# Four graph layers on one core: a unit of the score pass with all four tiles in rounded products, and two high-part buffers for three

## The chip, the core and the metric

One Trainium2 chip, one of its cores. The metric is device time in microseconds (us) of one execution. The core has five engines with an instruction stream each: TensorE (PE, matmuls; its weight loads show as PEld), VectorE (DVE), ScalarE (ACT), GpSimd (POOL) and SyncE (SP, which here only issues DMA). An engine runs its stream in order, and the streams are tied together by semaphores that this kernel sets and waits for by hand.

## What is computed

`x` is 4096 nodes by 128 features, `adj` a 4096 x 4096 matrix. Four graph layers follow each other, each with a layer norm and relu ahead of it and a residual sum behind it. The change lies in the fourth. Its parts that matter:

```python
node_adj_norm = node_adj.at[idx, idx].add(-dn)            # adj without its diagonal
node_support = node_adj_norm @ h                          # 4096x4096 @ 4096x128, the node-feature product
edge_output = _gru_cell(node_support, h, edge_Wih, edge_Whh, edge_bih, edge_bhh)
# per attention head:
hp = (node_adj > 0) @ hW
hm = (node_adj < 0) @ hW
e_plus = leaky_relu(concat([hp, hm]) @ a); e_minus = leaky_relu(concat([hm, hp]) @ a)
...                                                       # softmax over columns, weighted sum, second gated cell
return de[:, None] * edge_output + dn[:, None] * node_output
```

## The kernel before

**Tiles.** The 4096 output columns are cut into C = 8 chunks of 512 (`c`), the 4096 rows summed over into G = 8 units (`g`) of four tiles of 128. A unit is one 1 MB block of `adj` (128 x 2048 float32: four tiles of 128 x 512), loaded by SP into one of the slots of `ring`. Unit number n = 8c + g. The passes over `adj` are: degrees, the first two layers (`agg0`, `agg1`), the third (`gat`), then for the fourth the **score pass** (`edge` in names), a normalising pass (`norm`) that reads stored masks, and the output pass (`out`). Only the score pass is touched.

**One unit of the score pass.** PE needs two products of the unit. The first, of the sign masks with a small table, is eight narrow matmuls (`L1693`). The second is the node-feature product: one tile of four (the first, `WHOLE = 1`) as a plain float32 matmul of `ring` with `reg1` (`L1700`, which the trace records as two instructions a tile), and three tiles as three rounded (fp32r) products each, high x high, low x high and high x low (`L1705`, `L1706`, `L1707`). The other engines make the operands:

- ACT `L694` (`sign_of`): the sign of 128 x 2048 elements, from which the masks are made, two units ahead.
- ACT `L709` (`high_parts`): a rounded copy of the tiles that are multiplied in rounded products, one unit ahead, into one of `HIGHS` buffers in `a_hi`.
- DVE `L1206` (`low_parts`): what the rounding left, unit minus high part, into `a_lo`, which lies over `ring`.
- DVE `L1191` and `L1194` (`masks`): plus and minus masks from the signs, two units ahead, into one of four buffers. SP stores them to HBM for the `norm` pass and loads the unit n + 6.

A high-part buffer comes free when PE has finished the unit that read it:

```python
if n >= HIGHS:
    act.wait_ge(s_mm["edge"], n - HIGHS + 1)      # L707, L708
act.activation(edge_hi(n), ring[...], ACT.Copy)   # L709
```

**Work beside the units.** For each finished chunk a chain of small steps is woven into the next chunk's units, at fixed places. ACT and DVE do in step n the high and low parts of unit n + 1 *first*, then the small steps, then signs and masks of unit n + 2:

- ACT at g = 1: `candidate` of chunk c - 1 (`L747`), then `keep_edge` of chunk c (`L729`, `L732`: sums out of the banks). At g = 7: two gate tanh (`L741`, `L742`).
- DVE at g = 0: `cell_in` (`L1231` to `L1233`); at g = 2: `edge_nodes` (`L1214` to `L1219`) and `cell_end` (`L1241` to `L1245`); at g = 4: `result` (`L1258`).
- PE behind unit g = 0: `turn_edge` (`L1716`), which waits for `L729`; behind g = 2: `turn_cells` (`L1503`), which waits for `L1245`; behind g = 4: `gates` (`L1731` to `L1734`), which waits for `L1258`.

`turn_edge` exists from chunk 1 on, the steps that work on the chunk before (`candidate`, `cell_in`, `cell_end`, `turn_cells`, `result`) from chunk 2 on. Chunk 0 has instead the rounding of `h` (`L705` on ACT, `L1202` on DVE), once per unit. On the diagonal unit (g = c) DVE also clears four 128 x 128 blocks (`L1169`). The order is written out by hand; no scheduler moves anything.

Of the kernel before, what the change touches and what calls it, by code (L numbers as in the profile page):

```python
# [34 lines left out]
VCOLS = 3 * HEADS * WINDOWS  # L35
ECOLS = 3 * 2 * HEADS + 1
EPAD = 32
WHOLE = 1
SCORES = 2 * HEADS
RING_EDGE = 6  # L40
RING_OUT = 4
MASKS = 4
MLOADS = 8
HIGHS = 3
TILES = 7
AHEAD = 2
EARLY = T - 2 * Q
# [51 lines left out]
def build(nc, x_d, rows_d, cols_d, diag_d, w_d, gru_d, col_d, row_d, masks_d, lines_d, xs_d, hs_d, out_d):  # L99
    with ExitStack() as ctx:  # L100
# [117 lines left out]
        signs = [b[:, 0:UNIT // 4] for b in (hT, outT)]  # L218
        SPLIT = (Q - WHOLE) * W

        def edge_hi(n):

            first = (MASKS - 1) * UNIT // 2 + (n % HIGHS) * SPLIT
            return a_hi[:, first:first + SPLIT]
# [147 lines left out]
        def ring_at(p, g, off=0, size=UNIT, c=0):  # L372
            slot = (c * G + g) % SLOTS[p]
            return slice(slot * UNIT + off, slot * UNIT + off + size)
# [159 lines left out]
        def _(act):  # L534
# [162 lines left out]
            def high_parts(n):  # L697
# [5 lines left out]
                if c == 0:  # L703
                    act.wait_ge(s_hkept, g + 1)
                    act.activation(h_hi[:, g * W:(g + 1) * W], reg1[:, g * W:(g + 1) * W],  # L705
                                   ACT.Copy).then_inc(s_hhi, 1)
                if n >= HIGHS:  # L707
                    act.wait_ge(s_mm["edge"], n - HIGHS + 1)  # L708
                act.activation(edge_hi(n), ring[:, ring_at("edge", g, WHOLE * W, SPLIT, c=c)],  # L709
                               ACT.Copy).then_inc(s_ehi, 1)  # L710
# [167 lines left out]
        def _(dve):  # L878
# [318 lines left out]
            def low_parts(n):  # L1197
# [6 lines left out]
                dve.wait_ge(s_ehi, n + 1)  # L1204
                rest = ring_at("edge", g, WHOLE * W, SPLIT, c=c)
                dve.tensor_tensor(a_lo[:, rest], ring[:, rest], edge_hi(n).bitcast(F32),  # L1206
# [292 lines left out]
        def _(pe):  # L1499
# [175 lines left out]
            def edge_unit(n):  # L1675
# [20 lines left out]
                for q in range(Q):  # L1696
                    t = g * Q + q
                    part, tile = ring_at("edge", g, q * W, W, c=c), slice(t * P, (t + 1) * P)
                    if q < WHOLE:
                        pe.matmul(nacc[:, :], reg1[:, tile], ring[:, part], start=t == 0, stop=False)  # L1700
                        continue
                    if q == WHOLE:
                        pe.wait_ge(s_elo, n + 1)
                    hi = edge_hi(n)[:, (q - WHOLE) * W:(q - WHOLE + 1) * W]
                    pe.matmul(nacc[:, :], h_hi[:, tile], hi, start=t == 0, stop=False)  # L1705
# [214 lines left out]
```

## Time and profile before

| | us |
|---|---|
| runs | 2068.22 (median of 3; 2066.27 to 2068.49) |
| the profiled execution | 2069.2 |
| its span, first to last instruction | 2067.4 |
| score pass within the span | from about 912 to 1205 |
| PE busy over the span | 1848.6 (89%) |
| DVE busy | 1662.5 (80%) |
| ACT busy | 1482.7 (72%) |

PE is the busiest engine, at a mean granted clock of 0.98. The stages have different limits, so the share over the span says little on a change to one stage; it is read from the score pass's own rows. In a row of the timeline the start and the duration of an instruction are given, and in brackets the idle time of its engine ahead of it with what ended it. Matmuls overlap: the pace of PE is the distance of two starts, not the duration of one.

### The profile page before, as it was taken

How to read it: one execution, taken by the hardware profiler on the slowest of the kernel's cores; microseconds unless marked ns; L12 is line 12 of the kernel's file. 1: busy time of each engine (PE TensorE's matmuls, PEld its weight loads, DVE VectorE, ACT ScalarE, POOL GpSimd, SP SyncE). 2: the span in 40 equal slices, each digit the busy share in tenths (PEclk: the TensorE clock that was granted, in tenths of full speed). 3: DMA queues.
4: the chain of work that ended last, by engine and by line, in shares of the span. 5: the costliest groups of instructions: out<-in, count | busy, mean ns of one | idle time of the engine just before them, and what ended most of it. 6: DMA issues, size and time to landing. Idle time of an engine off the chain costs nothing.

```text
span 2067.4 us, 22984 instructions
## 1 busy us (share of the span) xinstructions
PE 1848.6 (89%) x8237; PEld 1243.8 (60%) x8237; DVE 1662.5 (80%) x2326; ACT 1482.7 (72%) x1824; POOL 13.3 (1%) x15
## 2 busy tenths in 40 slices
PE   2335999789998999989999989989999999999998
PEld 1223888568887999975555546645555555554554
DVE  4658988698886888887887863399898898989987
ACT  3445666456667999988877730199898898988984
POOL 0000000000010000000000000000000000000000
PEclk9999999899998999989999999999999999999999
DMA  9999898578884776659998969723334333335230
GB/s 389 429 428 387 324 342 340 197 279 317 317 318 181 263 257 247 257 180 360 353 352 338 352 230 394 246 97 112 112 128 133 137 114 116 117 113 167 97 97 21
DMA packets 84161, 497.96 MB, mean 241 GB/s; under 512 B 8737, under 2 KB 12834, under 8 KB 38738
## 3 DMA queue, kind: packets, MB, share of 16 engines
q1 hardware_dynamic: 79730, 494.33, 63.8%
q10 hardware_dynamic: 4320, 2.20, 0.4%
q8 instruction: 64, 1.05, 0.2%
q14 instruction: 47, 0.39, 0.1%
HBM read 456.55 MB, written 39.94 MB: 240 GB/s over the span
## 4 chain that ended last, share of the span: by engine, by line
PE 60%; DVE 15%; ACT 11%; DMA 8%; issue 5%; SPq 0%; DVEq 0%; ACTq 0%
PE bank L1814 17%; DMA ring<-in_adj_rows 7%; PE bank L1626 5%; PE bank L1628 5%; PE bank L1627 5%; PE bank L1788 4%; ACT work L682 4%; ACT work L677 3%; PE bank L1700 2%; PE bank L1822 2%; PE bank L1821 2%; PE bank L1823 2%; DVE work L1468 2%; DMA ring<-masks 2%; DVE a_lo L1048 1%
## 5 line engine op out<-in xcount | busy, mean ns | idle before, releaser
L1814 PE MATMUL bank<-work,reg 128*128 128x512 f32 x760 | 362.0, 601 | 14.3 <-DVE ring L1419 7.9
L833 ACT ACTIVATE work<-x,e 128x512 f32<-128x512 f32 x552 | 355.1, 709 | 0.4 <-PE bank L1823 0.4
L1468 DVE TENSOR_TENSOR work<-work,ring 128x1536 f32<-128x1536 f32 x184 | 322.1, 1754 | 9.2 <-ACT work L833 9.0
L1048 DVE TENSOR_TENSOR a_lo<-ring,a_hi 128x2048 fp32r<-128x2048 f32 x128 | 292.5, 2302 | 30.9 <-ACT a_hi L626 30.1
L626 ACT ACTIVATE a_hi<-ring 128x2048 fp32r<-128x2048 f32 x128 | 244.3, 1913 | 77.1 <-PE bank L1628 77.1
L1660 PE MATMUL bank<-reg,ring 128*128 128x129 f32 x2048 | 244.4, 282 | 25.2 <-DVE ring L1162 24.8
L1660 PEld LDWEIGHTS bank<-reg,ring 128*128 128x128 f32 x2048 | 239.4, 197 | 29.5 <-DVE ring L1162 19.0
L1814 PEld LDWEIGHTS bank<-work,reg 128*128 128x128 f32 x760 | 143.6, 191 | 137.0 <-issue 112.8
L1626 PE MATMUL bank<-a_hi,s_hi 128*128 128x512 f32 x512 | 207.4, 405 | 20.5 <-DVE a_lo L1048 20.5
L1628 PE MATMUL bank<-a_hi,s_lo 128*128 128x512 f32 x512 | 202.1, 395 | 0.0
L1627 PE MATMUL bank<-a_lo,s_hi 128*128 128x512 f32 x512 | 200.8, 392 | 0.0
L1821 PE MATMUL bank<-s_lo,h_hi 128*128 128x512 f32 x240 | 189.1, 788 | 2.7 <-DVE a_lo L1447 2.4
L1162 DVE SCALAR_TENSOR_TENSOR ring<-ring,work 128x2048 f32<-128x2048 f32 x64 | 147.3, 2302 | 40.1 <-ACT work L682 40.0
L1447 DVE TENSOR_TENSOR a_hi<-work,s_lo 128x512 fp32r<-128x512 f32 x172 | 118.9, 691 | 42.0 <-ACT s_lo L843 41.8
L843 ACT ACTIVATE s_lo<-work 128x512 fp32r<-128x512 f32 x172 | 106.6, 620 | 55.9 <-PE bank L1823 39.0
L558 ACT ACTIVATE work<-ring 128x2048 f32<-128x2048 f32 x32 | 61.1, 1910 | 101.2 <-DMA ring<-in_adj_rows 101.2
L682 ACT ACTIVATE work<-work 128x2048 f32<-128x2048 f32 x64 | 122.4, 1912 | 14.1 <-DVE work L1131 8.4
L1206 DVE TENSOR_TENSOR a_lo<-ring,a_hi 128x1536 fp32r<-128x1536 f32 x64 | 112.4, 1756 | 21.4 <-ACT a_hi L709 19.1
L1626 PEld LDWEIGHTS bank<-a_hi,s_hi 128*128 128x128 f32 x512 | 97.4, 190 | 42.5 <-issue 24.2
L1788 PE MATMUL bank<-ring,work 128*126 128x512 fp8e4 x512 | 115.3, 383 | 5.7 <-issue 3.9
L709 ACT ACTIVATE a_hi<-ring 128x1536 fp32r<-128x1536 f32 x64 | 94.6, 1478 | 35.6 <-PE bank L1707 35.5
L1628 PEld LDWEIGHTS bank<-a_hi,s_lo 128*128 128x128 f32 x512 | 96.9, 189 | 22.8
(273 smaller groups left out, 3045.3 us busy)
## 6 DMA issues: line engine op xcount, KB each, us to landing
ring<-in_adj_units SPq DMA_DIRECT2D x320, 1024.0 KB, 4.9
ring<-in_adj_rows SPq DMA_DIRECT2D x32, 2048.0 KB, 17.0
ring<-masks SPq DMA_DIRECT2D x64, 512.0 KB, 5.1
masks<-work SPq DMA_DIRECT2D x48, 512.0 KB, 9.0
masks<-ring SPq DMA_DIRECT2D x16, 512.0 KB, 9.0
x<-lines SPq DMA_DIRECT2D x8, 768.0 KB, 9.8
ring<-lines SPq DMA_DIRECT2D x8, 768.0 KB, 8.0
h_kept<-reg SPq DMA_DIRECT2D x1, 2048.0 KB, 14.4
```

The costliest lines, as they stand in the source:

```text
L626: act.activation(a_hi[:, (g % 4) * UNIT:(g % 4 + 1) * UNIT], ring[:, ring_at(p, g)], ACT.Copy).then_inc(s_ahi[p], 1)
L682: act.activation(gunit(n), gunit(n), ACT.Exp).then_inc(s_gexp, 1)
L833: last = act.activation(tiles(n)[:, k * W:(k + 1) * W], guard(c, k), ACT.Sigmoid, bias=e6[:, t * SCORES + k:t * SCORES + k + 1], scale=-1.0)
L1048: dve.tensor_tensor(a_lo[:, ring_at(p, g)], ring[:, ring_at(p, g)], a_hi[:, (g % 4) * UNIT:(g % 4 + 1) * UNIT].bitcast(F32), ALU.subtract) ...
L1468: dve.tensor_tensor(tv, tv, spread(ring[:, ring_at("out", g, q * W, W)], HEADS, 1), ALU.mult).then_inc(s_y, 1)
L1626: pe.matmul(acc[:, :], sh, hi, start=begin, stop=False)
L1627: pe.matmul(acc[:, :], sh, lo, start=False, stop=False)
L1628: last = pe.matmul(acc[:, :], sl, hi, start=False, stop=end)
L1660: last = pe.matmul(gat_acc(c, i), y[:, q * W + i * P:q * W + (i + 1) * P], xw[:, m, :], start=m == 0 and i % 2 == 0, stop=m == T - 1 and i ...
L1788: last = pe.matmul(bank[c % 2][0:VCOLS, :], table[:, t * VCOLS:(t + 1) * VCOLS], mask[:, q * W:(q + 1) * W], start=t == 0 and table is vp, ...
L1814: return pe.matmul(bank[1 + k][:, :], reg1[:, t * P:(t + 1) * P], tiles(c * T + t)[:, k * W:(k + 1) * W], start=t == 0, stop=t == T - 1)
L1821: pe.matmul(acc, h_hi[:, h], high, start=t == 0, stop=False)
```

## The change

Two constants change:

```diff
-WHOLE = 1
+WHOLE = 0
...
-HIGHS = 3
+HIGHS = 2
```

`WHOLE = 0`: no tile goes through the plain float32 product any more; the high copy (`L709`) and the low part (`L1206`) cover 2048 columns in place of 1536, and PE makes 12 rounded products a unit in place of 9 and the plain one. The wait for the low part now stands ahead of the first tile (`if q == WHOLE: pe.wait_ge(s_elo, n + 1)`), and not behind the plain one. `HIGHS = 2`: two buffers of 2048 columns lie where three of 1536 lay (4096 columns in place of 4608), and the high copy of unit n waits until PE has finished unit n - 2, where it waited for unit n - 3.

On PE this is one unit of the score pass, before (-) and after (+); `a_hi` holds the high part of `adj`, `a_lo` its low part, `h_hi` and `h_lo` those of the features:

```order
 L1693 MATMUL bank<-work 32x512 x4
 L1693 MATMUL bank<-work,reg 32x512 x4
-L1700 MATMUL bank<-ring,reg 128x512
+L1705 MATMUL bank<-a_hi,h_hi 128x512
+L1706 MATMUL bank<-a_lo,h_hi 128x512
+L1707 MATMUL bank<-a_hi,h_lo 128x512
 L1705 MATMUL bank<-a_hi,h_hi 128x512
 L1706 MATMUL bank<-a_lo,h_hi 128x512
```

The plain product is gone from each of the 64 units, and three rounded ones stand in its place. All else on PE keeps its place.

On ACT these are the instructions around the head of a chunk (steps g = 0 and g = 1), first before:

```order
L709 ACTIVATE a_hi<-ring 128x1536 [waits edge_unit_multiplied]
L694 ACTIVATE hT<-ring 128x2048 [waits edge_masks_made,unit_loaded2]
L709 ACTIVATE a_hi<-ring 128x1536 [waits edge_unit_multiplied]
L747 ACTIVATE ring<-ring 128x512 [waits edge_gates_steps]
L729 ACTIVATE hn<-bank 128x512 [waits edge_sum_turned,edge_unit_multiplied]
L732 ACTIVATE ring<-bank 128x512 [waits edge_gates_multiplied]
```

and after:

```order
L709 ACTIVATE a_hi<-ring 128x2048 [waits edge_unit_multiplied]
L694 ACTIVATE hT<-ring 128x2048 [waits edge_masks_made,unit_loaded2]
L709 ACTIVATE a_hi<-ring 128x2048 [waits edge_unit_multiplied]
L747 ACTIVATE ring<-ring 128x512 [waits edge_gates_steps]
L729 ACTIVATE hn<-bank 128x512 [waits edge_sum_turned,edge_unit_multiplied]
L732 ACTIVATE ring<-bank 128x512 [waits edge_gates_multiplied]
```

Nothing moves on ACT (nor on DVE, where `L1206` alone grows to 2048 columns). What changes besides the width is a number that these rows don't show: the second `L709`, the copy for unit 8c + 2, waits for unit 8c in place of unit 8c - 1.

## Rows read from the trace of the kernel before

**Rows 1.** Stretch; busy us of PE, PEld, DVE, ACT, POOL; clock, DMA share, GB/s.
```profile
1016.00:1053.00 37.00, 36.64 (x186) 20.69 (x185) 28.67 (x43) 29.03 (x22) 0.00 (x0) 1.00 0.90 342
```

**Rows 2.** Groups by line, 905 to 1210: busy and mean ns, idle before, releaser.
```profile
L709 ACT ACTIVATE a_hi<-ring 128x1536 fp32r<-128x1536 f32 x64 | 94.6, 1478 | 35.6 <-PE bank L1707 35.5
```

**Rows 3.** Timeline of PE, one unit: start and duration in us.
```profile
1092.95 0.40 PE L1693 MATMUL bank<-ring,work 128*32 128x512 fp8e4 x4
1093.49 1.13 PE L1700 MATMUL bank<-ring,reg 128*128 128x512 f32 x2
...
1094.69 0.39 PE L1706 MATMUL bank<-a_lo,h_hi 128*128 128x512 f32 x1
...
1096.31 0.40 PE L1707 MATMUL bank<-a_hi,h_lo 128*128 128x512 f32 x1
1096.64 0.40 PE L1693 MATMUL bank<-work 128*32 128x512 fp8e4 x4
```

**Rows 4.** The page's costliest groups: the same operations at 2048 columns, in earlier passes.
```profile
L1048 DVE TENSOR_TENSOR a_lo<-ring,a_hi 128x2048 fp32r<-128x2048 f32 x128 | 292.5, 2302 | 30.9 <-ACT a_hi L626 30.1
L626 ACT ACTIVATE a_hi<-ring 128x2048 fp32r<-128x2048 f32 x128 | 244.3, 1913 | 77.1 <-PE bank L1628 77.1
```

**Rows 5.** Timeline of all engines at the head of chunk 5, then chunk 6.
```profile
1096.88 0.42 DVE L1231 TENSOR_SCALAR ring<-ring 128x512 f32<-128x512 f32 x1
1098.91 0.63 ACT L747 ACTIVATE ring<-ring 128x512 f32<-128x512 f32 x1 [0.56 <-DVE ring L1233]
1099.44 0.58 ACT L729 ACTIVATE hn<-bank 128x512 f32<-128x512 f32 x1
1100.24 0.96 PE L1716 MATMUL bank<-select,hn 128*128 128x19 f32 x8
...
1136.61 0.96 PE L1716 MATMUL bank<-select,hn 128*128 128x19 f32 x8
```

**Rows 6.** Timeline at units g = 2 and 3 of chunk 5.
```profile
1105.39 0.18 DVE L1214 COPY esum<-bank 128x24 f32<-128x24 f32 x1
1106.32 0.69 DVE L1241 TENSOR_TENSOR ring<-reg,ring 128x512 f32<-128x512 f32 x1
1108.38 0.42 DVE L1191 TENSOR_SCALAR work<-hT 128x512 int32<-128x512 int32 x1
1108.52 0.65 PE L1503 MATMUL bank<-ident,ring 128*128 128x128 f32 x4
```

**Rows 7.** Timeline at unit g = 4 of chunk 5 and the gates behind it.
```profile
1115.41 1.12 DVE L1258 SCALAR_TENSOR_TENSOR x<-bank,diag,x 128x128 f32<-128x128 f32 x4
1116.63 1.10 PE L1731 MATMUL bank<-ring,gru 128*128 128x512 f32 x2
1121.95 0.40 PE L1693 MATMUL bank<-work 128*32 128x512 fp8e4 x4
```

**Rows 8.** Timeline behind the gates of chunk 5: the high copy waits for PE.
```profile
1125.30 0.40 PE L1707 MATMUL bank<-a_hi,h_lo 128*128 128x512 f32 x1
1125.73 1.48 ACT L709 ACTIVATE a_hi<-ring 128x1536 fp32r<-128x1536 f32 x1 [3.88 <-PE bank L1707]
...
1128.26 1.91 ACT L694 ACTIVATE outT<-ring 128x2048 fp8e4<-128x2048 f32 x1
```

**Rows 9.** As rows 1: PE waits of 2.0 and 2.6 us, low stretches, full clock.
```profile
1367.65:1369.69 2.04, 0.00 (x1) 0.00 (x1) 2.04 (x3) 0.56 (x2) 0.00 (x0) 1.00 0.02 4
1370.96:1374.37 3.41, 3.41 (x7) 1.67 (x6) 3.41 (x5) 3.41 (x7) 0.00 (x0) 0.51 0.64 269
...
1343.06:1347.80 4.74, 0.00 (x0) 0.00 (x0) 1.75 (x1) 4.73 (x8) 0.00 (x0) 0.92 0.00 0
1348.90:1353.50 4.60, 4.60 (x8) 2.26 (x7) 4.00 (x5) 4.60 (x9) 0.00 (x0) 0.50 0.01 2
714.40:716.95 2.55, 0.00 (x0) 0.00 (x0) 2.52 (x5) 1.74 (x3) 0.00 (x0) 1.00 0.90 267
717.00:720.00 3.00, 3.00 (x27) 3.00 (x28) 3.00 (x4) 2.64 (x2) 0.00 (x0) 1.00 0.33 139
```

## Prediction, made before the changed kernel ran

> **What bounds the kernel now.** First the windows of the score pass, for the bound of this stage: in 37 us of it PE is busy 36.64, ACT 29.03 and DVE 28.67, at full clock and with the DMA engines at 0.90 [rows 1]. Then the groups by line, for the slack of the feeders: ACT's high copy stands idle 35.6 us over the stage, nearly all of it waiting for PE [rows 2]. So PE sets the pace and the feeders wait for it. Then the timeline of one unit on PE [rows 3]: from signs to signs 3.69 us; the plain tile and one rounded product take 1094.69 - 1093.49 = 1.20, and seven further products 1096.31 - 1094.69 = 1.62, so 0.231 each and 0.97 for the plain tile. Last the timeline at the three places where PE waits for a small step of another engine [rows 5 to 7], and behind the gates, where the copy waits for PE [rows 8]. A chunk lasts 1136.61 - 1100.24 = 36.4 us [rows 5].
>
> **What it removes.** 64 plain tiles of 0.97 become 64 times three products of 0.231: 0.27 saved a unit, 3.42 in place of 3.69. With PE alone that is 17.3 us.
>
> **What it adds on the feeders.** By the same operations at 2048 columns the copy takes 1.91 (1.48 now) and the low part 2.30 [rows 4], which at 1536 columns is about 1.76. ACT then has copy and signs, 3.6 us a unit (each next instruction starts 0.10 ahead of the end of the last one, as L729 behind L747 [rows 5]); DVE low part and masks, about 3.5. Both are now above PE's 3.42, but PE has 6.7 us of small steps a chunk besides (turn_edge, turn_cells, gates), so by sums alone the three are level near 34 us a chunk. Sums don't decide; the new wait does.
>
> **The new wait.** The copy of unit n + 2 may now start only when PE has finished unit n. From there to the products of n + 2: hand-over 0.03 (the end of L1707 to L709) [rows 8], copy 1.91, low part 2.30, hand-overs 0.1, so 4.3 us, and PE has unit n + 1 (3.42) and the signs of n + 2 (0.54) to do: it loses 0.4 where nothing lies between. That is the small part. The large part is queued behind the waiting copy. ACT and DVE run in order and do a unit's copy and low part ahead of the small steps, and these now start one unit later, while PE waits for them at the same place as before.
>
> I walked one chunk (c of 2 or more) with the durations above, t = 0 when ACT sees unit g = 4 of the chunk before as finished (0.43 behind the last product's start [rows 8]). In a steady state the gates start at 1.93 (third wait below) and last 5.3 [rows 7], so the signs of g = 5 start at 7.17, and this unit is finished at 10.69, g = 6 at 14.11.
>
> - g = 7 and g = 0. Copy of g = 7 at 10.69, low part done 14.94, products 0.45 late; finished 17.98. ACT is behind too: copy of g = 0 at 14.30, gates' tanh (2.53 from copy to signs less 1.38 [rows 8]), signs to 19.16. Low part of g = 0 done 18.55, products 0.19 late, finished 21.59.
> - **Turn_edge.** Copy of g = 1 at 19.06, its low part done 23.31, only then cell_in (23.23), and candidate 2.03 behind its start [rows 5], at 25.26. The copy of g = 2, which waited for the end of g = 0, stands ahead of it and is done at 24.59. Then L729, 25.79 to 26.37, and turn_edge at 26.41. PE could have started it at 21.39: 5.0 us idle. (Before, L1716 followed L729's end at 1100.02 by 0.2, with PE busy.) In chunk 1, without candidate, copy and L729 alone come to 2.6.
> - **Turn_cells.** Unit g = 1 is finished at 30.82; copy, low part to 35.07, edge_nodes 0.93 and cell_end 2.06 plus the tail of its last instruction [rows 6], PE at 38.12. PE was done with g = 2 at 34.14: 4.0 us idle.
> - **Gates.** g = 3 finished at 42.22; copy, low part to 46.47, result 1.12 [rows 7], gates at 47.57, where PE was free at 45.44: 2.1 us idle.
> - g = 4 is finished at 45.64. That is the new length of a chunk, 45.6 against 36.4.
>
> Clearing the diagonal falls where DVE has room in each chunk but chunk 2 (0.2 us). The stores of masks, which stopped DVE at places before, have more time per unit now.
>
> **Sum.** From gates of chunk 1 to gates of chunk 7: the first of these six stretches starts without a gates' wait, so 43.5 + 5 x 45.6 = 271.7, against 6 x 36.44 = 218.6 measured: +53.1. Chunk 0 and the head of chunk 1: in chunk 0 rounding h comes on top, ACT needs 0.52 + 1.81 + 1.80 = 4.1 a unit against PE's 3.7 now; with the 2.6 at turn_edge, two losses of 0.45 and 0.8 behind it, and the saving, +3.8. Tail: gates' wait of chunk 7, one late unit, and a last cell step 1.75 late, less three units' saving, +3.5. Together +60 us at full clock.
>
> **The clock.** [...] In 1 us windows past the first 380 us I find eight waits of 2.0 to 2.6 us, six of them followed by a low stretch, and all longer ones followed by one. 3.4 us at half clock lose 1.7 us of work at most, about 1.5 where part falls in a wait or on narrow work. Twelve waits of 4 and 5 us, three quarters of six of 2.1 and most of one of 2.6: (12 + 4.5 + 0.8) x 1.5 = 26; I take 23, since a second wait can swallow the end of a low stretch. Bounds: 0, and 19 x 3.4 us at half twice over, 19 x 3.4 = 65; I stay near the 2.04 us row.
>
> [...] The row of 714 us shows that one can go free.
>
> Against the profiled execution's own 2069.2 the sum is 2069.2 + 60 + 23 = 2152; that execution lay 1 us above the median of the runs, so against the median 2151.
>
> **Rivals.**
> 1. *Waits as walked, clock stays full*: 2069 + 60 = 2129. For it: one of the short waits was free. Against: all the longer ones weren't.
> 2. *Low clock lasts twice as long* behind the waits of 4 and 5 us, as it does behind the 4.7 us one [rows 9]: up to 12 x 1.5 = 18 more, 2170.
> 3. *The feeders catch up*: I have the copies and low parts of g = 1 to 5 always starting as late as their buffer allows and the helpers right behind. If the helpers came out only the copy's own time late (2.6 at turn_edge, near nothing at the other two), it were 2069 - 17 + 7 x 2.6 + clock 7 x 1.5 = 2081. Against: cell_end and result stand behind a low part that needs that copy, by program order.
> 4. *Faster*: the new buffer wait never binds and PE's saving goes through, 2069 - 17 = 2052. One mechanism: unit n + 2 must be ready 3.96 us behind the end of unit n, and turn_edge must find L729 done. It decides for this side if copy and low part together took under 3.9 (they take 4.2 in the page's rows) and if L729 didn't stand behind the copy; half of that by itself gives nothing.
>
> **Chances.** Forecast 0.62, rival 1 0.14, rival 2 0.14, rival 3 0.06, rival 4 0.02, and 0.02 for about no change by pieces of 3 and 4. The range takes in rivals 1 and 2 with the errors of the walk, 2120 to 2172. 0.2% (4 us) is what can be told from no change here. Faster 0.03, same 0.02, slower 0.95.
>
> **What would show it.** L1716 of neighbouring chunks 45 to 51 us apart; PE idle at L1716 (to L729 and L747) near 5 us six times and 2.6 once, at L1503 (to L1245) near 4 us, at L1731 (to L1258) near 2; L709 at 1.91 and L1206 at 2.30; unit spacing near 3.42 between waits; the granted clock of the stage below 0.95. Wrong if L1716 finds L729 done, if chunks come out below 40 us, or if the waits are there and the clock stays at 1.00.

## The result, and the profile after

The changed kernel takes 2177.19 us (median of 4; 2176.33 to 2179.17) against 2068.35 in the same session: 1.0529 times as long, interval 1.051 to 1.0547. That is 109 us slower, where +83 had been forecast, with 2172 as the upper end of the range. The side and the mechanism were right, the size fell short by 26 us.

The span is 2175.5 us at a mean granted clock of 0.958. Starts of the gates (`L1731`) cut the difference of 108.1 us between the two spans into three parts. Until the gates of chunk 1 it is 9.2 us (979.37 against 970.21), over the six chunks from there to the gates of chunk 7 (1294.43 against 1188.84) it is 96.4 us, and 2.5 us from there on. A chunk takes (1294.43 - 979.37) / 6 = 52.5 us, where it took 36.4.

First the groups by line, the rows that answer to [rows 2, 4]: mean duration of one, then idle time ahead of them.

```profile
L1206 DVE TENSOR_TENSOR a_lo<-ring,a_hi 128x2048 fp32r<-128x2048 f32 x64 | 146.5, 2290 | 126.3 <-ACT a_hi L709 126.2
L709 ACT ACTIVATE a_hi<-ring 128x2048 fp32r<-128x2048 f32 x64 | 121.9, 1905 | 128.2 <-PE bank L1707 128.1
```

Copy and low part cost what rows 4 had promised, and both idle more than before: the copy 128.2 us for 35.6, the low part 126.3. More work per unit, and more idle time: so the wider operations are not what they are short of. The copy waits for PE, the low part for the copy. Next the waits of the score pass (engine and line, what it waited for, us in total, times, longest), for where PE waits in turn:

```profile
ACT a_hi L709 <- PE bank L1707: 128.1, 23, 8.8
...
PE bank L1716 <- ACT hn L729: 31.6, 7, 5.1
...
PE bank L1503 <- DVE ring L1245: 24.7, 7, 3.9
...
PE bank L1705 <- DVE a_lo L1206: 13.4, 14, 6.5
PE bank L1731 <- issue: 11.5, 6, 2.0
```

Before, PE's waits at L1716 and L1503 came to 1.6 and 1.0 us. Now it waits for the small steps at the three places of the walk. One chunk's three places in the timeline, in the order of time, answer to [rows 5 to 7]:

```profile
1159.63 1.90 ACT L709 ACTIVATE a_hi<-ring 128x2048 fp32r<-128x2048 f32 x1
...
1161.42 0.75 DVE L1233 SCALAR_TENSOR_TENSOR ring<-bank,gb,ring 128x512 f32<-128x512 f32 x1
...
1162.21 0.63 ACT L747 ACTIVATE ring<-ring 128x512 f32<-128x512 f32 x1 [0.67 <-DVE ring L1233]
1162.74 0.58 ACT L729 ACTIVATE hn<-bank 128x512 f32<-128x512 f32 x1
...
1163.37 1.90 PE L1716 MATMUL bank<-select,hn 128*128 128x19 f32 x8 [4.77 <-ACT hn L729]
...
1170.23 1.91 ACT L709 ACTIVATE a_hi<-ring 128x2048 fp32r<-128x2048 f32 x1 [4.62 <-PE bank L1707]
1172.17 2.29 DVE L1206 TENSOR_TENSOR a_lo<-ring,a_hi 128x2048 fp32r<-128x2048 f32 x1 [5.28 <-ACT a_hi L709]
...
1176.76 0.69 DVE L1245 SCALAR_TENSOR_TENSOR ring<-ring 128x512 f32<-128x512 f32 x1
1177.50 0.66 PE L1503 MATMUL bank<-ident,ring 128*128 128x128 f32 x4 [3.82 <-DVE ring L1245]
...
1188.62 1.90 PE L1731 MATMUL bank<-ring,gru 128*128 128x512 f32 x2 [1.90 <-issue]
```

The copy of g = 2 stands ahead of L747 and L729 and ends at 1161.53. What ends last is cell_in on DVE, behind the low part of g = 1: L747 idles 0.67 us for its last instruction, L1233, and L729 follows. Both queues hold turn_edge, and PE idles 4.77 us there. Then copy and low part of g = 3 stand ahead of the cell steps, 3.82 us at turn_cells; last 1.90 at the gates, behind result. The walk had 5.0, 4.0 and 2.1, and 2.6 for chunk 1, where 2.59 was measured. The eight narrow matmuls of L1716 take 1.90 us here, at a granted clock of 0.50, and took 0.96 at 1.00. The windows right behind two of the waits (columns as rows 1):

```profile
1158.70:1163.30 4.60, 0.00 (x0) 0.00 (x0) 4.50 (x7) 3.93 (x5) 0.00 (x0) 0.80 1.01 412
1163.40:1167.80 4.40, 4.40 (x20) 3.23 (x21) 3.15 (x3) 2.21 (x2) 0.00 (x0) 0.50 0.45 169
...
1107.50:1109.20 1.70, 0.00 (x0) 0.00 (x0) 1.67 (x4) 1.14 (x3) 0.00 (x0) 0.50 0.97 371
1109.20:1117.90 8.70, 8.67 (x37) 5.90 (x37) 4.01 (x7) 2.74 (x3) 0.00 (x0) 0.55 0.29 121
```

Behind the first wait the clock is at 0.50 for the whole 4.4 us; behind the one of the chunk before it stays low through nearly 8 us of work. The pace of units where nothing waits, PE's signs of two successive ones in the timeline, answers to [rows 3]:

```profile
1147.56 0.40 PE L1693 MATMUL bank<-work 128*32 128x512 fp8e4 x4
...
1151.05 0.40 PE L1693 MATMUL bank<-ring,work 128*32 128x512 fp8e4 x4
```

That is 3.49 us, not 3.42. The first rounded product behind the signs starts at 1148.11 and the next one at 1148.44, 0.33 us apart where the others are 0.23 apart. My 0.231 was read from products further back in a unit, so about 0.2 us a unit is saved where I had 0.27.

On the clock again. Read off in windows of 1 us, every one of the 19 waits of 1.9 us and more from chunk 1 to the gates of chunk 7 is followed by a low stretch, at 0.50 of full. Nine of these are 3.4 us long, eight 6.8 and two 10.2, 105 us together, part of it still in the wait. I had priced 17.3 stretches of 3.4, 59 us.

### The profile page after: what moved, and what is told of

The parts are those of the page before. It is cut to its first block, busy times and chain, and to the rows that moved or that the text cites. A ratio compares the mean times of both kernels' runs of the same rounds, so it can differ in the third digit from the quotient of the medians.

```text
span 2175.5 us, 23112 instructions
## 1 busy us (share of the span) xinstructions
PE 1876.8 (86%) x8301; PEld 1277.0 (59%) x8301; DVE 1695.0 (78%) x2326; ACT 1510.3 (69%) x1824; POOL 13.3 (1%) x15
## 4 chain that ended last, share of the span: by engine, by line
PE 56%; DVE 17%; ACT 14%; DMA 8%; issue 5%; SPq 0%; DVEq 0%; ACTq 0%
PE bank L1814 15%; DMA ring<-in_adj_rows 6%; PE bank L1626 5%; PE bank L1628 5%; PE bank L1627 5%; PE bank L1788 4%; ACT work L682 4%; ACT work L677 3%; ACT a_hi L709 2%; PE bank L1705 2%; DVE a_lo L1206 2%; DVE work L1468 2%; PE bank L1822 2%; PE bank L1821 2%; PE bank L1823 2%
## 5 line engine op out<-in xcount | busy, mean ns | idle before, releaser
L1048 DVE TENSOR_TENSOR a_lo<-ring,a_hi 128x2048 fp32r<-128x2048 f32 x128 | 292.4, 2301 | 31.0 <-ACT a_hi L626 30.1
L626 ACT ACTIVATE a_hi<-ring 128x2048 fp32r<-128x2048 f32 x128 | 244.3, 1913 | 76.5 <-PE bank L1628 76.5
L1206 DVE TENSOR_TENSOR a_lo<-ring,a_hi 128x2048 fp32r<-128x2048 f32 x64 | 146.5, 2290 | 126.3 <-ACT a_hi L709 126.2
L709 ACT ACTIVATE a_hi<-ring 128x2048 fp32r<-128x2048 f32 x64 | 121.9, 1905 | 128.2 <-PE bank L1707 128.1
L1705 PE MATMUL bank<-a_hi,h_hi 128*128 128x512 f32 x256 | 119.0, 465 | 13.5 <-DVE a_lo L1206 13.4
```

What stands on the lines that cost most here:

```text
L626: act.activation(a_hi[:, (g % 4) * UNIT:(g % 4 + 1) * UNIT], ring[:, ring_at(p, g)], ACT.Copy).then_inc(s_ahi[p], 1)
L1048: dve.tensor_tensor(a_lo[:, ring_at(p, g)], ring[:, ring_at(p, g)], a_hi[:, (g % 4) * UNIT:(g % 4 + 1) * UNIT].bitcast(F32), ALU.subtract) ...
```

## Experiments

### Is it the buffers or the rounding? buffers_only

```diff
 # the kernel before
-HIGHS = 3
+HIGHS = 2
```

> The kernel before with two high-part buffers of 1536 columns in place of three, nothing else. My theory: the buffer wait alone puts the small steps behind a late copy. Walked with 1.48 and 1.76 us for copy and low part: PE waits 3.5 us at turn_edge, 2.8 at turn_cells, 0.9 at the gates, so a chunk takes 43.2 us in place of 36.4; with some 4 us of low clock a chunk the kernel takes about 2137 us, 2125 to 2150. Rival (the wider copies and low parts are what costs, ACT and DVE having become the bound): within 5 us of before.

2133.36 us (2132.48 to 2136.9), ratio 1.0324, interval 1.0309 to 1.034: 66 us slower, with the widths of before. In its trace PE waits 3.36 us at L1716 in five chunks (4.09 in chunk 2), 2.7 at L1503, 0.76 at L1731; the walk had 3.5, 2.8 and 0.9. A chunk takes 47.0 us. That is the 43.2 of the walk and the 4 that I had allowed for the clock. So the number of buffers by itself makes 66 of the 109 us, and the rival on wider operations as the whole cause falls. The rest, 44 us, comes when the operations ahead of the small steps grow by 0.43 and 0.54 us on top.

### Is it the queue behind the late copy? steps_first, all_steps_first

```diff
 # ACT, step g, in all_steps_first (steps_first: keep_edge alone moved)
+if c > 1 and g == 1: candidate("edge", c - 1)
+if c and g == 1: keep_edge(c)
 if 2 <= n + 1 < C * G: high_parts(n + 1)
-if c > 1 and g == 1: candidate("edge", c - 1)
-if c and g == 1: keep_edge(c)
 # DVE, step g (steps_first: all but cell_in moved)
+edge_nodes, cell_in, cell_end, result at their g
 if 2 <= n + 1 < C * G: low_parts(n + 1)
-edge_nodes, cell_in, cell_end, result at their g
...
```

> The changed kernel (two buffers of 2048 columns) with the small steps written ahead of the waiting copy or low part: keep_edge ahead of the copy at g = 1, edge_nodes and cell_end ahead of the low part at g = 2, result ahead of it at g = 4. My theory, the queue behind the late copy: the three waits of PE fall below 1 us each, 0.5 to 1 us a chunk is lost on late low parts, clock near 1.00, the kernel about 2065 us (2055 to 2080). Rival, the buffer loop itself (copy, low part, products of two units): it stays above 2120.

> steps_first, and cell_in ahead of the low part at g = 0 and candidate ahead of the copy at g = 1 as well; two buffers of 2048 columns. In steps_first PE still waited 3.7 us at each turn_edge, now for cell_in, behind a low part of a late copy. If that is the same queue, the wait goes and with it its low clock: 2102 - 6 x (3.7 + 1.9) = about 2068 us (2060 to 2076). If the buffer loop itself is the limit, it stays above 2090.

steps_first: 2102.25 us (2099.68 to 2103.17), ratio 1.0166, interval 1.0152 to 1.018, so 75 us of the 109 are gone by order alone, with two buffers and wide operations. The waits at L1503 and L1731 have vanished. It came out above my 2080: I had overlooked that turn_edge also waits for cell_in, which had stayed behind its low part. One of its rows:

```profile
1082.62 1.87 PE L1716 MATMUL bank<-select,hn 128*128 128x19 f32 x8 [3.73 <-DVE ring L1233]
```

all_steps_first moves that too: 2092.95 us (2092.26 to 2094.34), ratio 1.0127, interval 1.0113 to 1.0142. The gain of 9 is a quarter of the 34 that I expected. Its waits over the pass show what is left:

```profile
PE bank L1705 <- DVE a_lo L1206: 16.0, 20, 5.3
PE bank L1716 <- ACT hn L729: 14.6, 7, 2.9
```

PE now waits for low parts at more places, and 2.2 us at L1716 in most chunks, since ACT reaches candidate and L729 late behind copies and signs of its own (1114.01 to 1116.32 in the trace: signs, L747, L729 with no gap between them worth naming). A chunk takes 39.6 us. Of 52.5 - 36.4 = 16.1 us a chunk, order takes away 12.9, and 3.2 are left with two buffers and wide operations in this order.

### Would three buffers save it? three_buffers, five_slots_only

The third buffer of 2048 columns takes a slot of the ring; so the control has the shorter ring alone.

```diff
 # three_buffers, from the changed kernel
-HIGHS = 2
+HIGHS = 3
-RING_EDGE = 6
+RING_EDGE = 5
...
+if n % HIGHS == 2: return a_lo[:, 5 * UNIT:6 * UNIT]      # in edge_hi
```

> The changed kernel with three high-part buffers of 2048 columns; the third takes the place of the sixth unit slot of the ring, so units are loaded five ahead. My theory: no wait of PE at turn_edge, turn_cells and gates, clock at 1.00 in the pass, a chunk 34.5 to 35 us, the kernel 2058 us (2051 to 2066), faster than before. Rival (wider copies and low parts as the bound): well above before, 2100 or more. Rival on the loads: one slot less makes ACT or DVE wait for units, seen as waits for the loads.

> The kernel before (plain tile, three high-part buffers of 1536) with units loaded five ahead in place of six: the control for three_buffers. If the sixth slot costs nothing, 2067 to 2070 us, and the 18 us that three_buffers took over before belong to the wider copies and low parts. If the loads are the cause, 2075 or more, with ACT waiting for units.

five_slots_only: 2069.87 us (2066.48 to 2079.33), ratio 1.0021, interval 1.0008 to 1.0035, so with the operations of before the slot costs about 0.2%, although ACT now waits 21 us for loads over the pass, where it waited 0.4. three_buffers: 2085.34 us (2084.61 to 2090.08), ratio 1.0086, interval 1.0072 to 1.0099. The third buffer takes back 92 us of 109, but my theory expected a gain of 9 over before and got a loss of 18. In its trace PE still waits at the small steps, in one chunk 1.62 us at L1718 (the L1716 of this file), 1.30 at L1505 and 1.41 at L1733. I read this as feeders so slow that one unit of lead doesn't cover the small steps, but the rival on the loads has a part too, which the control with its narrower operations can't show. In chunk 2, 43.3 us long where the next five take 38 to 39.5, the diagonal clearing waited for a load, ACT's signs waited 3.61 us behind it, and PE came to wait 5.15 at turn_edge, with the clock at 0.50 for 6.8 us behind (998.6 to 1005.4):

```profile
992.20 0.90 DVE L1171 TENSOR_TENSOR ring<-ring,offdiag 128x128 f32<-128x128 f32 x4 [3.14 <-DMA ring<-in_adj_units]
...
998.53 1.89 PE L1718 MATMUL bank<-select,hn 128*128 128x19 f32 x8 [5.15 <-ACT hn L731]
```

That is some 5 of the 18 us that the six chunks of this trace lose. How the rest divides between wide operations and loads isn't shown.

### Both cures, and order alone on the kernel before

> Both cures: three buffers of 2048 columns and all small steps ahead of the copies and low parts. The three engines need about 34 to 35 us a chunk each by sums. If order was what was left of the loss in three_buffers, about 2060 us (2053 to 2068), faster than before. If DVE and ACT are the bound with the wider operations, 2070 to 2085, about as three_buffers.

> The kernel before with all small steps ahead of the copies and low parts, nothing else. PE is the bound there and finds the small steps done, so nothing should change: within 3 us of before. If it is faster than that, the small steps cost time before, too.

three_buffers_steps_first: 2069.35 us (2067.47 to 2073.72, 11 runs), ratio 1.0014, interval 1.0005 to 1.0023, between the two ranges that I had written. before_steps_first: 2063.65 us (2061.12 to 2065.34, 11 runs), ratio 0.9979, interval 0.997 to 0.9988: 3.7 us faster than before, a small gain that I had not expected (35.9 us a chunk for 36.4), and the fastest kernel of the study. The windows over five chunks of each, the rounded one first (columns as rows 1), show what the plain tile buys:

```profile
1007.75:1188.66 180.91, 173.60 (x921) 110.31 (x920) 162.53 (x212) 158.54 (x105) 0.00 (x0) 1.00 0.92 350
```

```profile
1004.39:1183.65 179.26, 179.26 (x881) 103.56 (x880) 143.43 (x215) 141.09 (x104) 0.00 (x0) 1.00 0.92 351
```

PE is busy 5.7 us less of five chunks with 12 rounded products, and no time comes of it: DVE and ACT have 19 and 17 us more to do, and PE isn't busy 100% any longer. In five chunks it waits 5.6 us for low parts of units, and ACT 5.7 us for loads. No engine is full (DVE 90%, the DMA engines at 0.92 in both), so which of these closes the gap last stays open. The two kernels also differ by the sixth slot, which cost 2.5 us in five_slots_only, and no run has the rounded products with six slots. What is shown is that PE's saving came to nothing in the form that was run.

### What does the clock cost? filled_waits and its two halves

```diff
+def filler(c, count):
+    if c > 1: pe.wait_ge(s_ga["edge"], 2 * (c - 1) - 1)      # bank 6 is free
+    for i in range(count):
+        pe.matmul(bank[6][:, :], h_hi[:, 0:P], h_hi[:, 0:W], start=True, stop=True)
 def turn_edge(c):
+    if c < C: filler(c, 19 if c > 1 else 10)                 # not in other_waits_filled
...
+filler(c, 15)                                                # not in edge_wait_filled
 turn_cells("edge", c - 1)
...
+if c > 1: filler(c, 7)                                       # not in edge_wait_filled
 gates("edge", c)
```

> The changed kernel; ahead of each of the three waits PE makes rounded products of resident tiles into a bank that is free then (19, 15 and 7, and 10 at the turn_edge of chunk 1), which are never read: it does 0.231 us of work each where it sat idle. The waits for ACT and DVE stay as they are. Theory, the clock was the term that I sized too small: granted clock back above 0.99 in the pass and 2129 to 2138 us, 40 to 48 us faster than the changed kernel. Rival (the walk at full clock was too short, and the clock costs the 23 us that I had given it): 2150 or more.

> The changed kernel with unread products only ahead of turn_edge (19, and 10 in chunk 1); the waits at turn_cells and gates stay empty. The low stretches behind the seven turn_edge waits sum to 54 of 105 us in the changed kernel's trace. If the price of a wait goes with the length of its low stretch, 2177 - 21 = 2156 us. Rival (each wait costs 1.5 us, whatever its length, as I had reckoned): 7 of 19 waits, 2177 - 15 = 2162 or more.

> The complement: unread products ahead of turn_cells (15) and gates (7), none ahead of turn_edge. By the length of the low stretches 2177 - 19 = 2158 us; by the count of waits (12 of 19) 2177 - 25 = 2152. If the parts add, both gains together are the 40 us of filled_waits.

filled_waits: 2136.91 us (2131.67 to 2138.47), ratio 1.033, interval 1.0314 to 1.0346. PE does more work, the small steps come no sooner, and the kernel is 40 us faster. One chunk of PE, and a window over five chunks:

```profile
1182.26 4.51 PE L1715 MATMUL bank<-h_hi 128*128 128x512 f32 x19
1187.20 1.07 PE L1725 MATMUL bank<-select,hn 128*128 128x19 f32 x8 [0.43 <-ACT hn L729]
1195.10 3.60 PE L1715 MATMUL bank<-h_hi 128*128 128x512 f32 x15
1199.09 0.66 PE L1503 MATMUL bank<-ident,ring 128*128 128x128 f32 x4 [0.39 <-DVE ring L1245]
1206.56 1.79 PE L1715 MATMUL bank<-h_hi 128*128 128x512 f32 x7
1208.72 1.10 PE L1740 MATMUL bank<-ring,gru 128*128 128x512 f32 x2 [0.37 <-issue]
```

```profile
1024.16:1254.85 230.69, 223.30 (x1125) 148.12 (x1126) 164.01 (x212) 159.81 (x106) 0.00 (x0) 1.00 0.74 268
```

The waits are full, L1716's matmuls (L1725 here) run at 1.07, and the clock is 1.00. 230.69 / 5 = 46.1 us a chunk: this is the kernel that the walk described, with 45.6.

edge_wait_filled: 2150.01 us (2145.71 to 2150.18); other_waits_filled: 2153.21 (2151.88 to 2156.03). The seven waits at turn_edge give back 27 us, 3.9 each; the twelve others 24 us, 2.0 each. (Before took 2069.14 in their session, 0.8 more than in that of the changed kernel, so each gain may be 1 us larger.) So the price is not one sum per wait, and my rival to that effect falls. My own sums by the length of the stretches, 2156 and 2158, were missed too, by 6 and 5 us, since they took the stretches behind the waits left empty as given. Nor do the parts add: 27 + 24 = 51, and both together gave 40. With turn_edge filled, the waits of 1.9 us at the gates of chunks 4 to 7 are followed by no low stretch (the clock is at 1.00), though in the changed kernel every one was; in chunks 2 and 3 each still has one of 3.4 us behind it. The gates of chunks 3 and 4 in edge_wait_filled:

```profile
1076.19 1.44 PE L1740 MATMUL bank<-ring,gru 128*128 128x512 f32 x2 [1.92 <-issue]
...
1125.54 1.10 PE L1740 MATMUL bank<-ring,gru 128*128 128x512 f32 x2 [1.92 <-issue]
```

The same wait, behind the same filled one, is paid in one chunk and free in the next. So a wait's price isn't its own alone, but what decides isn't shown: filling also shifts all later waits in time. What does go with the gains is the low time that is left. From the turn_edge of chunk 1 to the gates of chunk 7, in windows of 0.2 us, it is 105 us in the changed kernel, 34 with turn_edge filled, 51 with the others filled and none with both, so 27, 24 and 40 us were gained for 71, 54 and 105 us of low clock: 0.38 to 0.44 each.

## Why the prediction was off

- *What bounds the kernel, and what goes from PE*: right in kind; 0.2 us a unit is saved and not 0.27, some 12 us over 64 units and not 17. The feeders were taken a little too busy: in three_buffers_steps_first DVE is busy 32.5 us a chunk and ACT 31.7 against PE's 34.7, where I had all three near 34.
- *The new wait, and the three places behind it*: right, by place, releaser and size (4.8, 3.8 and 1.9 for 5.0, 4.0 and 2.1), and shown by buffers_only and by steps_first, which takes the same waits away without touching a buffer.
- *The new length of a chunk, 45.6 at full clock*: right, 46.1 in filled_waits. The 0.5 over the walk is about what eight units at 3.49 in place of 3.42 add; it wasn't taken apart further.
- *The clock, +23*: this is the step that failed. The term was mis-sized: filled_waits puts it at 2177.2 - 2136.9 = 40.3 us. "3.4 us at half clock lose 1.7 us of work at most" held for a stretch, but I gave each wait one stretch of 3.4 us by the row at 1371 us, and left the row at 1349 us, low for 4.6 us and more behind a wait of 4.7, to rival 2 with 0.14 [rows 9]. (By the timeline that wait was 5.8 us, 1342.06 to 1347.87; my window had cut it short.) Nor was it the only one: in the kernel before, three of the four waits of 3.5 to 6.0 us between 600 and 2050 us have a low stretch of 6.8 us. This is the one that ends at 658.9, in windows of 1 us (columns as rows 1):

```profile
656.00:657.00 1.00, 0.00 (x0) 0.00 (x0) 0.54 (x1) 1.00 (x5) 0.20 (x1) 1.00 0.60 74
657.00:658.00 1.00, 0.00 (x0) 0.00 (x0) 1.00 (x1) 0.91 (x3) 1.00 (x1) 0.77 0.87 360
...
663.00:664.00 1.00, 1.00 (x7) 1.00 (x7) 0.79 (x2) 1.00 (x2) 0.00 (x0) 0.50 0.00 0
664.00:665.00 1.00, 1.00 (x9) 1.00 (x9) 0.90 (x1) 1.00 (x2) 0.00 (x0) 0.82 0.00 0
```

Waits of 3.8 to 5.1 us were the rule here, twelve of the 19, and nine of them brought 6.8 us or more. I also counted a quarter of the short waits as free; none was. All 19 paid, with one stretch of 3.4 us each [rows 9], would come to 19 x 1.7 = 32 us by estimate; the 8 from there to the measured 40 I put down to the length of the stretches. Rival 2 had 23 + 18 = 41 for the clock, near the measured 40 though its doubling held for nine of the twelve longer waits only; its 2170 missed by 7, about what the walk was short.
- *Chunk 0 and the head of chunk 1, +3.8*: too small; it was +9.2, and +7.6 with the waits filled. I had walked chunk 0 by ACT's 4.1 us a unit and left out a small step of DVE ahead of a low part there, the same mistake in kind that the walk avoided elsewhere. At 945.09 the small operations of the third layer's projection (L1106 to L1115), with L1202 behind them, hold the low part of unit 7 until 947.44, and PE, whose signs of unit 7 were at 947.14, gets it at 949.77, with the clock at 0.50 for the 3.4 us behind. At the signs of unit 7 PE is 1.0 us behind the kernel before, at those of unit 8 it is 4.5.
- *The six chunks and the tail*: from gates to gates the walk has 6 x 45.6 - 218.6 = 55 and 1.4 behind them (the gates' wait of chunk 7 falls on the other side of that cut). filled_waits has 58 and 1.8, the changed kernel, with its clock, 96 and 2.5.
- *Rival 4, the saving goes through*: wrong even where its condition is nearly met. three_buffers_steps_first has a third buffer and no queue (its copies still wait 8.8 us for PE in five chunks), and does not beat before; I had called the sums of the three engines "level near 34 us a chunk" and had not asked what that leaves of a saving. Here it left nothing.

So 60 at full clock was 68 by the span of filled_waits (3.8 more ahead of chunk 1's gates, 3 in the chunks, the rest in the tail), and 23 was 40.

## What to carry to other kernels

When a buffer is dropped, look less at the loop that reuses it than at what stands in program order behind the instruction that now waits: helpers that a third engine needs are delayed by a whole unit, and writing them ahead of the waiting instruction gave back 84 of 109 us here. Count a saving on the busiest engine only as far as the next ones have room: with 0.2 us a unit less on PE and 0.97 more on the two feeders, nothing was won, though no feeder was busy more than 90% of the time. And price a wait of PE by the low stretches that waits of its own length left in the trace, since here the clock took 40 of 109 us.

## What the hardware showed that I had not expected

- Unread matmuls in PE's waits made the kernel 40 us faster, with 256 more rounded products.
- The low stretches came in lengths of 3.4, 6.8 and 10.2 us (nine, eight and two), and the two of 10.2 were both behind a wait at turn_edge, with PE's narrow matmuls (128 x 19) first in line behind it. Other waits of the same 4.8 us at the same place brought 6.8; what decides isn't shown.
- A wait of 1.9 us was followed by a low stretch in all six chunks of the changed kernel, and in only two of six when the wait at turn_edge, 24 us ahead of it, was filled with work.
